# A merged order of four strands rewritten, and passes of the identity put ahead of TensorE's work

## The reference

```python
def reference(x, ...):                      # x: (1, 2048, 128)
    for l in range(4):
        sa, ca, ga, sb, cb, gb = (silu(c[l]) @ wmod[l]).reshape(...)
        ga, gb = away_from_zero(ga), away_from_zero(gb)
        x = x + ga * attn[l](layernorm(x) * (1 + ca) + sa)
        x = x + gb * ffn[l](layernorm(x) * (1 + cb) + sb)
    return x
```

## Time and profile before

| | |
|---|---|
| plain runs, median of 3 (lowest to highest) | 1222.34 us (1215.33 to 1223.31) |
| profiled execution: time / span | 1225.84 / 1223.8 us |
| busy: PE / DVE / ACT / POOL | 1082.9 / 872.7 / 685.5 / 493.8 us |
| mean granted clock of TensorE | 0.926 |
| moved by DMA | 70.14 MB |

### The profile page before, as it was taken

One profiled execution on the slowest core, in us unless ns is written; L12 is line 12 of the kernel. 1 busy time (PEld: TensorE's weight loads), 2 busy tenths in 40 slices (PEclk: granted clock), 3 DMA queues, 4 the chain that ended last, 5 costly groups with the idle time before them and its releaser, 6 DMA issues.

```text
span 1223.8 us, 18281 instructions
## 1 busy us (share of the span) xinstructions
PE 1082.9 (88%) x6855; PEld 654.4 (53%) x6855; DVE 872.7 (71%) x2050; ACT 685.5 (56%) x1155; POOL 493.8 (40%) x475
## 2 busy tenths in 40 slices
PE   7999999899999899999999867779899987659978
PEld 5766544344444354456444313464568676338868
DVE  4745547567666768788799899675686989966446
ACT  4477566686745586655676724562525786544221
POOL 2014122212213520184246456525455465686363
PEclk9999999999999789999999868769799998869989
DMA  8103000000000000000000000000514043147583
GB/s 257 57 9 138 1 1 0 1 1 2 1 1 18 1 2 1 20 1 1 18 1 1 0 0 1 1 3 33 172 52 166 33 164 112 33 168 232 209 291 92
DMA packets 36071, 70.14 MB, mean 57 GB/s; under 512 B 3088, under 2 KB 26128, under 8 KB 35472
## 3 DMA queue, kind: packets, MB, share of 16 engines
q0 software_dynamic: 9680, 45.88, 10.6%
q1 hardware_dynamic: 26304, 23.10, 6.0%
HBM read 59.34 MB, written 9.63 MB: 56 GB/s over the span
## 4 chain that ended last, share of the span: by engine, by line
PE 60%; DVE 14%; POOL 8%; ACT 8%; issue 6%; DMA 2%; another core or an unknown queue 1%; DVEq 0%; SPq 0%; POOLq 0%; ACTq 0%
PE ps L899 9%; PE ps L2177 5%; PE ps L1477 5%; PE ps L2185 3%; DVE own L2035 2%; PE ps L861 2%; PE ps L673 2%; PE ps L1276 2%; PE ps L1751 1%; PE ps L659 1%; POOL own L2059 1%; POOL own L1721 1%; PE ps L1455 1%; PE ps L1754 1%
## 5 line engine op out<-in xcount | busy, mean ns | idle before, releaser
L899 PE MATMUL ps<-own,g_f 128*128 128x512 f32 x320 | 147.8, 602 | 0.1
L899 PEld LDWEIGHTS ps<-own,g_f 128*128 128x128 f32 x320 | 59.2, 191 | 67.2 <-issue 61.0
L1226 POOL TENSOR_TENSOR own<-own 128x512 f32<-128x512 f32 x32 | 40.1, 1254 | 131.1 <-PE ps L899 95.5
L2035 DVE TENSOR_TENSOR_SCAN own<-own,carry 128x512 f32<-128x512 f32 x48 | 77.7, 1618 | 15.5 <-POOL own L2059 13.6
L2059 POOL TENSOR_TENSOR own<-own 128x512 f32<-128x512 f32 x32 | 50.7, 1585 | 53.2 <-ACT own L1985 53.0
L1939 PE MATMUL ps<-own,g_c 128*128 128x512 f32 x64 | 44.5, 784 | 30.5 <-POOL own L2065 30.4
L1976 ACT ACTIVATE own<-own,Acol 128x512 f32<-128x512 f32 x64 | 45.2, 714 | 40.1 <-PE ps L1939 38.9
L1895 POOL TENSOR_TENSOR own<-own 128x512 f32<-128x512 f32 x32 | 44.5, 1392 | 55.7 <-DVE own L1869 35.9
L1477 PE MATMUL ps<-g_l,own 128*128 128x512 f32 x128 | 59.5, 611 | 7.7 <-issue 7.3
L531 ACT ACTIVATE own<-xs,sm 128x128 f32<-128x128 f32 x128 | 52.5, 483 | 24.0 <-POOL sm L523 24.0
L2399 DVE TENSOR_TENSOR own<-ps,own 128x512 f32<-128x512 f32 x53 | 36.1, 682 | 41.4 <-PE ps L2177 13.3
(11 more groups left out here) (498 smaller groups left out, 2984.7 us busy)
## 6 DMA issues: line engine op xcount, KB each, us to landing
so<-own SPq DMA_DIRECT2D x10, 256.0 KB
g_l<-p_l SPq DMA_DIRECT2D x1, 2449.0 KB, 13.4
own<-sx SPq DMA_DIRECT2D x9, 256.0 KB, 9.5
g_f<-p_f SPq DMA_DIRECT2D x1, 2223.5 KB, 10.6
...
```

The source lines that it names most:

```text
L899: x = e.matmul(s.bank["V%d%d%d" % (it, k, cc)][:, :], ew2[:, m, 128 * cc:128 * cc + 128], gm, start=False, stop=m == 3)
L2035: e.tensor_tensor_scan(H, A, H, init, ALU.mult, ALU.add).then_inc(*s.dve.up("H%d" % n))
```

## The change

`ORDER` is replaced by another string of the same length, with the same number of each letter. A second string, `PASSES`, has a digit for each of the 1061 calls of `hold`, in the order in which they come. In `hold`, after the wait for the bank and before the bank is given to the caller, TensorE multiplies the identity by itself so many times and writes the product to the first 128 columns of the bank, where the caller's own matmul overwrites it later. The digits add up to 437 passes; 150 calls have any, and the most is 9. `Banks` gets the identity matrix for it.

```diff
--- before.py
+++ after.py
@@ -31,44 +31,57 @@
 NAMES = ["L0A", "L0F", "L1A", "L1F", "L2A", "L2F", "L3A", "L3F"]
 ENGINES = {"pe": "abcde", "act": "fghij", "dve": "klmno", "pool": "pqrst", "sp": "uvwxy"}
 ORDER = (
-    "ttyyyojkkokpopepplpfooooaolaqnfqlfmaqqafnmgasfraaraakkkeqksnmkkkffsksrksirrkafdfaaaaiofohddkkakaeefkkffkiicoahaaoocchjhd"
...
-    "dnndinrddidrrdnnddindndnndddidndndddimdndndddixsssssssmmdnmmdndwddidddsnnnddnnndnnnx"
+    "ytytyojkkpkoopepplfpllqomaqaofnqqfagqnsmmnosaoforrafaaaakrekkrrhskskkkskfkfikaacofodffhaiaakkihakaddfkkafkfaakikakadfkja"
...
+    "dicnnccchndmdmiddididncnncndsmdmiwddididnsnnnddisddidsidnsxxnnsndsdirddirdidnrnxnsndrddirdirdndnsnddidirdnrddnndsidnddsn"
+)
+
+
+PASSES = (
+    "000000000000000000000000000000000000000000000000000000000000000000000000000000000000000000000000000000001000000000000000"
+    "000000000000000110000000000000100000000000000000000000000000000000000000007000000000000000111000103000000000000000030000"
+    "000000000000000000000000000000000000000000000000000000000000000000000000000000000000000000011100030211335451000000001201"
+    "400230020700000000000000004000011014791000000000000002000000000131000020000002000000000000000000000000000000311010000000"
+    "000000000000000000000000000000000000000000000000000000000000010000000000000109331000010000000000000000000023000000000000"
+    "003020465206000000002030040094610220001000000521404317053900000000000000010300400003210603585306600490000000000000000000"
+    "000000000000000000000000000000000000000000000000000000000000000000000000000000000000000004000000000002000000000000000000"
+    "000000000206100415000000000000000000200000000000320020111000000000000000100230020012000114300221623692010210130000005000"
+    "10000000400220000000000000000001000000000000000000000000500000000010000000000000000000000000000000000"
 )
 
 
@@ -135,12 +148,12 @@
 class Banks:
 
 
-    def __init__(self, banks):
-        self.banks = banks
+    def __init__(self, banks, ident):
+        self.banks, self.ident = banks, ident
         self.begin()
 
     def begin(self):
-        self.free, self.let_go = list(range(8)), {b: () for b in range(8)}
+        self.free, self.let_go, self.passes = list(range(8)), {b: () for b in range(8)}, iter(PASSES)
 
     def hold(self, s, q, name, *steps):
         b = min(self.free, key=lambda b: max([step.turn(at) for step, at in self.let_go[b]], default=-1))
@@ -150,6 +163,8 @@
             q.wait_ge(*step(at))
         self.let_go[b] = steps
         s.bank[name], s.number[name] = self.banks[b], b
+        for _ in range(int(next(self.passes))):
+            q.eng.matmul(self.banks[b][:, 0:128], self.ident, self.ident, start=True, stop=True)
         return self.banks[b]
 
     def take(self, s, q, name, *steps):
@@ -232,7 +247,7 @@
         TILES = [0, (4 * W + 8 * 127) // 128, NJ, NJ]
         sx = [None] + [nc.dram_tensor(f"sx{c}", (TILES[c] * 128, D), F32, kind="Internal").ap() for c in range(1, NC)]
         so = [None] + [nc.dram_tensor(f"so{c}", (TILES[c] * 128, D), F32, kind="Internal").ap() for c in range(1, NC)]
-        banks = Banks([ctx.enter_context(nc.psum_tensor(f"ps{i}", [128, W], F32)) for i in range(8)])
+        banks = Banks([ctx.enter_context(nc.psum_tensor(f"ps{i}", [128, W], F32)) for i in range(8)], V["ident"])
 
         wmod = G["l2"][:, 0:3072].rearrange("p (l n) -> p l n", l=4)
         stage = G["l1"][:, 0:512].rearrange("p (h n) -> p h n", h=4)
```

More of the change, by code:

```diff
@@ L38 @@
[L38 to L61, removed]
@@ new lines @@
+    "aaagllflambbrbrffafrfaagrkkhakakfkdfbfndlfaanagkgkkdkkblagndfbbnffbnnfagafaaaibfddldfakiapkafkafdkdikakgddkakiaafqakdfid"
+    "dkidkdnnlaannnldkdlddinqaiqnnndqpddiqgdaaibkiiagaafapaaffakfaapfkkakkdpcdhddnndndfndnfdnddfenniniodfdtodoidkidkiikddkddi"
+    "kidkdkaainanfdfafaaffadkdikdkaanapikasfknaafflqnqafnasfssbfsbbgaagiaafaaapfaaafgfbkbgbbllbgglbgllagglbblfpllblkbbgkaaggk"
+    "kgkagkkgaaapalaafllflfalfkfbpbblbkbgbkbgqaaklkallkkbbpgdlbibblbbgbgfblffbbfqfblkbbbqbbkgkbkgkglbgqbkkglblkalalfaqfafaafa"
@@ new lines @@
+    "gagkgkkfagkkcrccrhkclpphhlchlccphplfclclhalpbfbmhmamhamgmagmfkbfkfccgbfhaagmbbmgmfmbmfcflcflaffclhlhhbbbqfkhkfbkkhfbbfkh"
+    "cmbgmmbgmgglgamgmfaafcccmfbchmfrcfahckkkfaaamacffckhbmfmcfccccckgkkffhkchmarfaafkcckfkfamffaacfkfkkkcchcrcchfchmfkharhfc"
+    "mcfmfamafcmffkkkfraakfbkfkkaabkhkaaqbbkgabbhkbbkgkhgkkalhbgmflalqlbblllbmlmkbbbqbbbgmmgmgckcglchmbkhphpcgppbbqflllahbllh"
+    "flagqccgkkgckfkgakmfakgakfamkalamkcccrkkklfcfmllfcclhklchlhhlchkkmbbkhkkgbkgbgbbgafbalfakklcclabcgkabkclccchlrccchhlqhqa"
@@ new lines @@
+    "mqqgakkkkqkakhkkammmammbcmggkkkkkbkkrkallkkkbkkbkgkkaggbcckkkkkkkubukggkcgpmpglggplccpcgcklrccflgpagmcgflfhaarhakhakhakh"
+    "aakakmccmkfkapmkcfmpbmkhaahkfbfkpgbhpmafgahkpgagrkfgakphbafmgapmgfmbbgpmggkaggmfplbbllbakmaflmpmkcchckhclhllcchlfcfpbmgp"
+    "amgbmallgbbkcbhbklgckgglgkgglllbggkglbbglblkblgmggldsgmddsgglllblbfdmlkrirbkblarniibrdlhllddldlinrcnbiinhdgncnhibmicmflc"
+    "lhddhldhiqccqhnncaqnhqngndmkdkdihbkiidgppdhbhhmpippblhlmgblhmgbfllllghlllimhblligngblllllgblglabfnblgnalbkkkdfkbbkiklbsl"
@@ new lines @@
+    "nkbnlllllblllnbkkllcnhlchllhlclhlkhckhmcmmhhccmcdhbmnhmmhclhlhllhmhclclhmcmmhhblmhmhmmcblhhmccllhllcchmlchlcmmhalhhmdvva"
+    "mhmldhdinhdmdinccidddmdiamlafflnaqqkdkqkqgkcckdkkqamfnscbmmfddmgmgmacnbbhkpbklcflbmbmbbmblrdrllrlbrhsladalgiaqikagflqaib"
+    "kgakqilaakpikaflafpbkbgkakgqaffckaphkalfqaafagkakqkaafpkfckpakfmbkmbphllbhbgcqgmmbmmqamhclfbbmglgqlddddqgbmlqdgnbsnmddnq"
+    "mmabhnmhmalammllclchlalmdmgmkckckfcllhcpnhbcgmsmbmalilicckilcmqkqicmmqmqmgqkcmpmpmmbmmcgpmpmmfmmcmnnpamcfmnmmcmmmnanakka"
@@ new lines @@
+    "nfandmdfmmmdfkbmmimlmilwdwliddillbifmdmagbfllrlrlllrrhnbbnbngcrngddldhlshkdkffkflddlilldiliikbikkbgbbllbgqkbgblglblbqblg"
+    "lbglbqlgbblgblqlbglabbgqnbllgblaagkaaqfaakaacpfkfkafkfkfdkpbbfkpkiaaakadkfbmlblffkdfilbpfbkgbkpdglqaalaaglbkfqdkddasfdfk"
+    "bfidlpfddiliplqkianaqaakqdfqkffngnaasnddfnqknpaakdpfnkaksibdkfkddffkafidnpfdiakdgkpikibnbllbngbnandgklgngbnsaagnddflsflf"
+    "lgglgaaalfdlplkpabikakffbblfflbgibqlibkgbilbgiklclggbkbgqblqkgcmnbblbaglffalgpgblgnpcnbaqlqlgblbnggnglcmlbbglqbmgqblclbl"
@@ new lines @@
+    "gnbgglgnbqblqgkfmkcnplclammbkbhmagrlggblbbglbqdkiqdllgdidkiddildkdblppbmbcgpbppmfhlhgrgglgcrnqnanqbflcildhlbmrmbgbaggchl"
+    "gcrgnqlcncqnblsskmgssilhkdhskiikqfdmdmrdirdbinihdnlirmdicicinchniicrnikmbinhcildrimiididnhimrdiidiicniddnndinnhidnnriidn"
+    "dnidnldidciniilniqqindnnimqqiidndgndnmmdkkikbikminiimngidnnmdinbinhndldlndlngnnnndllllilmdmcnnbhnsclsllmssimmdllrlrildrl"
+    "rhrdlqnndnnqnidnicqndhindqnnncnqidmndinqnnndmiqncnicqimdnqhnnddqmmqdnmqmmmdnnqnnndqnnnqmmdnnqnnndqqnnnqdnnvvvnvvvnqncnch"
@@ new lines @@
+    "nqnhcmmdmmbnmbgbmgcmgncnccmhncmhcnnrhncxnhxcnbmbgsmsgbmbbrgmnhccmshscrimcmbmhshcbbgcrglcmbhmcmldrhbiciqclddmdnhdmndnddnd"
+    "nndincnsbbbginbsbbdqngidnscidsmhidlsnccdridnsncisbdilndscndisndidsilccmscnhbhdqimbbmsmbgmbhrldmqlcnbbrnnbgncnbnlvmbbiqlb"
+    "lnbgnbbqmdglbilbldmqlbbnrnbgrbnrbbrslhslbvsbsgriclbblsqbhdqbicgqdlmcnndmhndincncnhnncnhbbnnhbmldhmidimdnhhnhbnbbngqmbngd"
+    "ninddmindnsdinndinsdnidndidsmmdndinndidsmdnndinddisldnndinddislldndninddisdnnccdincsmccchmcccrbdmhqmhcbnhhnbhmcrgmcrmbmc"
@@ new lines @@
+    "hmcchmmchhmhcrbhmbmrbcqmglncvlbshsmccblslhhsmcbbqhibrmblrmhbbgscmmgccqclchlbhbmhhbqmhbrdlgblmvricmccmcchdldnhnhbmhbidrhm"
+    "dilrmdibqcnimcmicnhcichnhmhbibrimbhnbrmgcqmgbnhmcclhbhnmhbbqlhblrgnbmbbrnddmdgclhbmldidrblvnscllbbmcngbimdmibdlddmdlnrdr"
+    "bnrrhlvndninichqnicismmsmhndqmnqdimdmnqdiidmminqcsinsmndqnnqdmimdqidmimdmimpmsmnsindnrrldidridindinrnsilsllndlrvnrndidnr"
+    "ididnirsnisnwwwwdrrnnrdicrindidchrdhnciphcscchcishndpmccpnicnpcinipdccichsndshnidrmimcnpccmsmchcmrdmrnccpchcmdrmwnccnchn"
```

16 lines of the change are left out of this document (4 added, 12 removed).

## The result

The changed kernel takes 1245.4 us (median of 4, 1239.0 to 1257.2) against 1220.1 (median of 4) for the kernel before: 1.022 times as long, with a 95% interval of 1.014 to 1.031. Taken again with more runs, it is 1.025 (1.021 to 1.030). The forecast was 1204 us. The clock did what was expected of it, and the time did not follow.

What follows compares the result with a forecast made beforehand. TensorE was taken to bound the kernel, with DVE full in 690:765. From 1225.8 us, -19 (clock), +9 (passes) and -8 (order) gave 1207.8; with plain runs 3.5 us under the profiled one, 1204, range 1176 to 1232.

Steps and rivals of the forecast that it cites:

- the +9 for the passes: Delay in us from 138 passes without an operand wait, 30.8 us of work, taken at 0.3; ends 0 and 39.
- the -8 for the order: Gain in us expected from the new step order closing waits for other engines; ends -25 and +15.
- the rise of the clock: TensorE's mean clock was to go from 0.926 to about 0.96, and over 0.85 in 690:765 and 765:823.
- the 16.3 us: Most that a full clock could save on the chain in 400:450, 690:765, 765:823 and 1055:1100 together.
- The rival of the transposes: Passes run but, like transposes, don't raise the clock; 1235 us, chance 0.05.
- the -19: Gain in us from the higher TensorE clock over the whole kernel; ends 0 and -34.
- 154 of 292: Of 292 passes without an operand wait, those before L3A's B and C rows, counted as hidden behind full DVE; 34 us if uncovered.
- the 124 and 16 of the prediction: 124 passes with an operand wait in the same step and 16 alone in a step, counted as free.
- the four stretches: 400:450, 690:765, 765:823 and 1055:1100: 259 passes, 57.8 us, were to just fit 62.1 us of TensorE idle time.
- The +15: Bad end, in us, of the order's term: a reshuffle can open waits as well as close them.
- Rival 1: Passes without an operand wait delay the strands at 39 us, giving 1234, or 1242 in a worse case; chance 0.14.
- Rivals 2 and 4: 2: clock gain lost in DVE, GpSimd and late data, 1219 us, chance 0.22; 4: all works, 1176 us, chance 0.14.

Runs made afterwards that it cites:

- the splices: Five kernels without passes, following one order up to letter 1907, 3279, 3490 or 3700 and the other behind it; 0.9986 to 1.0089 of the kernel before.

## Why the prediction was wrong

Two terms of the sum failed: the +9 for the passes, and the -8 for the order. The bound and the rise of the clock were right.

*What bounds the kernel* was read rightly: PE, and DVE in 690:765, where on the old order a clock of 0.93 in place of 0.75 bought nothing. PE's shares of the chain by stretch were read too low, since the lists of the earlier trace rows break off: over the whole stretches they are 64% in place of 49 and 52% in place of 43, and the 16.3 us become 20.

*The clock.* That the passes lift it, and where, was right: 0.95 and 0.97 in 690:765 and 765:823, 0.973 over the span, over the 0.96 expected. The rival of the transposes falls with it: the passes alone took the clock on the new order from 0.920 to 0.963. The Trainium skill's rule (TensorE: Matmul & The Clock Gate, Part 4) speaks of transposes, and the identity issued as a matmul is not under it by these traces. What the clock is worth was not too high either in 400:450, where 4.9 us were counted and some 7.5 came. But in 765:823, where 7.3 us were counted, passes at 0.85 and 0.88 took the steps to 56.6 and 55.1 us against 56.1 to 59.1 without, and neither kernel was faster at its end (1.004 and 1.003). How much of the -19 came cannot be told, as no run has the clock without the passes.

*The price of the passes* was mis-sized. 0.223 us a pass was exact. The weight wasn't: I set 154 of 292 at nothing, the 145 others at nothing too (the 124 and 16 of the prediction leave out five of them), and 138 at 0.3 of their price, 9 us in all. In 450:620 of the old order, where PE was busy 94% of the time, all 45 cost their whole price, whether an operand wait followed or not. The mistake was to compare the passes outside the four stretches (39.7 us) with PE's idle time outside them (78.8 us) over 996 us of run, and not step by step: the four matmuls of L1F1 that get 21 passes ran back to back, with no idle time between them. Nor did the passes inside the four stretches just fit: in 765:823 alone 74 of them, 16.5 us, met 10.9 us of idle time. On the new order it is there that the lasting loss begins (24 passes, 6.8 to 12.8 us), while the early one is mostly taken up again; why the old order doesn't take it up stays open. Clock and passes together were forecast at -10 us and measured at +17.5 on the new order and +32 on the old.

*The order* was the worst step: -8 forecast, +14 and +19 measured by the medians on two chips. I took the passes' place as a sign that the plan behind the order followed this kernel, and gave it a gain that no row showed. The +15 that I had set as its bad end was what came. Which steps cause it stays open; the splices place it before letter 1907 and between 3490 and 3700. Nothing in the trace of before said that the order was poor; and six table reloads fewer, the one part with a price, are real and cost or save nothing that shows.

*The rivals.* Rival 1 came nearest in time (1234 to 1242) and half in mechanism: passes on a full PE are paid for. It left out the order, which is as large. Rivals 2 and 4 needed an order that does no harm. The range's upper end had no room for a bad order and paid passes together, though each was a case of its own.
